# Second attention phase: the maxima's rows are transposed, copied and sent one position sooner in the pair ahead of theirs

## What is computed

```python
q = (x @ Wq.T + bq).reshape(b, l, h, hd).transpose(0, 2, 1, 3)      # k, v alike
scores = jnp.where(causal, jnp.einsum('bhqd,bhkd->bhqk', q, k) / math.sqrt(hd), -jnp.inf)
out = jnp.einsum('bhqk,bhkd->bhqd', jax.nn.softmax(scores, axis=-1), v)
return out.transpose(0, 2, 1, 3).reshape(b, l, d) @ Wo.T + bo
```

## Time and profile before

| | us |
|---|---|
| median of 3 runs | 1889.95 |
| lowest and highest run | 1889.94, 1899.09 |
| profiled execution, its own time | 1892.44 |
| span of the profiled execution | 1890.7 |
| PE busy in the span | 1665.3 (88%) |
| DVE, ACT, POOL busy | 1098.8, 861.6, 644.7 |
| mean granted TensorE clock | 0.947 of full |

### The profile page before, as it was taken

The page is one execution under the profiler, slowest core; times in us unless marked ns, Lnnn a source line. Parts: engine busy times, 40 slices in busy tenths (PEclk is TensorE's granted clock), DMA queues, the critical chain, the costliest instruction groups (busy, mean ns, idle before and its releaser), DMA issues. The chain is left out here.

```text
span 1890.7 us, 31907 instructions
## 1 busy us (share of the span) xinstructions
PE 1665.3 (88%) x10736; PEld 1162.3 (61%) x10736; DVE 1098.8 (58%) x2394; ACT 861.6 (46%) x1530; POOL 644.7 (34%) x1926
## 2 busy tenths in 40 slices
PE   4889988989986999999578899889889878999997
PEld 4555655655644777877455566566466446777785
DVE  5677677677763854545455655654654627554542
ACT  3456546555553544535234443443443426354441
POOL 4445545445440312213124433433433412131211
PEclk8899999999988999999789999899899898999998
DMA  2000110100105410110433533433443326211010
GB/s 102 2 13 14 41 30 13 35 24 13 35 24 168 128 67 12 55 67 1 150 48 49 78 57 68 75 51 68 74 63 63 52 86 193 70 37 67 0 45 23
DMA packets 78121, 106.97 MB, mean 57 GB/s; under 512 B 13195, under 2 KB 49675, under 8 KB 77973
## 3 DMA queue, kind: packets, MB, share of 16 engines
q1 hardware_dynamic: 77972, 105.10, 23.2%
HBM read 62.34 MB, written 16.78 MB: 42 GB/s over the span
## 5 line engine op out<-in xcount | busy, mean ns | idle before, releaser
L242 PE MATMUL f_ring<-xt,f_codes 128*128 128x512 f32 (+1 forms) x1408 | 362.6, 400 | 13.9 <-DVE f_codes L1519 7.9
L242 PEld LDWEIGHTS f_ring<-xt,f_codes 128*128 128x128 f32 (+1 forms) x1408 | 264.6, 189 | 84.0 <-issue 8.7
L1433 POOL TENSOR_TENSOR f_ht<-f_work,f_ht 128x512 fp32r<-128x512 f32 (+1 forms) x88 | 114.5, 1305 | 519.6 <-ACT f_ht L1491 519.6
L859 ACT ACTIVATE aa_region<-aa_scores 128x512 f32<-128x512 f32 x320 | 184.6, 599 | 83.5 <-PE aa_scores L1152 80.5
L859 ACT ACTIVATE ab_region<-ab_scores 128x512 f32<-128x512 f32 x320 | 181.4, 601 | 79.6 <-PE ab_scores L1152 79.1
L1576 DVE TENSOR_TENSOR f_work<-f_ring,f_work 128x512 f32<-128x512 f32 (+1 forms) x176 | 120.6, 690 | 139.8 <-ACT f_work L1480 117.2
L712 POOL TENSOR_SCALAR_AFFINE_SELECT ab_region<-ab_region 128x128 f32<-128x128 f32 x512 | 140.2, 297 | 176.7 <-ACT ab_region L859 176.2
L1480 ACT ACTIVATE f_work<-f_ring,f_scales 128x512 f32<-128x512 f32 (+1 forms) x176 | 120.6, 685 | 171.0 <-PE f_ring L242 170.5
L242 PE MATMUL f_ring<-f_dcodes,f_ht 128*128 128x512 f32 (+1 forms) x704 | 174.4, 402 | 9.7 <-DVE f_down_x L1546 9.2
L712 POOL TENSOR_SCALAR_AFFINE_SELECT aa_region<-aa_region 128x128 f32<-128x128 f32 x512 | 136.6, 295 | 91.8 <-ACT aa_region L859 91.4
L1112 PE MATMUL ab_maxima<-ab_stacks 96*128 96x128 bf16 (+3 forms) x512 | 144.9, 320 | 25.7 <-DMA ab_stacks<-ab_parted 13.4
(11 more groups left out here) (183 smaller groups left out, 2943.6 us busy)
## 6 DMA issues: line engine op xcount, KB each, us to landing
ab_stacks<-ab_parted SPq DMA_DIRECT2D x192, 128.0 KB, 4.2
f_raw<-mid SPq DMA_DIRECT2D x32, 256.0 KB, 4.4
f_x<-mid SPq DMA_DIRECT2D x28, 256.0 KB, 4.0
f_raw<-in_gate_q SPq DMA_DIRECT2D x10, 512.0 KB, 5.5
f_raw<-in_up_q SPq DMA_DIRECT2D x10, 512.0 KB, 4.6
f_raw<-in_down_q SPq DMA_DIRECT2D x10, 512.0 KB, 3.8
aa_x<-in_x SPq DMA_DIRECT2D x18, 256.0 KB, 2.8
ab_x<-mid SPq DMA_DIRECT2D x18, 256.0 KB, 3.0
```

Source lines behind the costliest of these rows:

```text
L242: mm = pe.matmul(out, w, x, start=start and i == 0, stop=stop and i == len(pairs) - 1)
L859: act.activation(probs[:, s // 2 % 2, SUB * (s % 2) + i, :], scores[:, sbk, :], ACT.Exp, scale=0.25).then_inc(scores_freed[sbk].sem, 1)
L1433: pool.tensor_tensor(ht[0:r, LO, n, :], hid[0:r, n % 2, :], ht[0:r, HI, n, :].bitcast(F32), ALU.subtract).then_inc(hid_lo.sem, 1)
```

## The change

In `ab` the positions at which the rows are transposed (PE), copied (DVE) and sent (SP) go from 2 to 1. In `aa` they stay at 2. No instruction is added or removed.

```diff
-        TRANSPOSE_AT, ROWS_AT, VALUES_AT = 2, 2, 4
+        TRANSPOSE_AT, ROWS_AT, VALUES_AT = (2, 2, 4) if rope else (1, 1, 4)
```

## The result

The changed kernel takes 1909.16 us in the median (1897.55 to 1914.72, 14 runs) against 1894.16 (1886.92 to 1899.76, 14 runs) before: ratio 1.0077, 95% interval [1.0062, 1.0092]. That is 0.8% slower, and outside the range of the prediction. The profiled execution took 1902.98 us, 10.5 more than that of before and the third quickest of the 14.

The account below looks back on a forecast made before the run. PE was taken to set the pace, with at most its 22.6 us wait for the maxima's rows removable. Step terms summed to +4.0 us, plus +2 for the clock: 1898.4 for the profiled execution, median 1896 us, range 1886 to 1906.

Parts of the forecast that it names:

- the low clock spreads: Rival: PE falls to the low clock in some eight steps with new or longer waits, 1907.6 us; chance 0.22.
- the term for the clock: Second attention phase: one or two more low-clock stretches at 1.7 us each, +2 us, bounds 0 to +14.
- the split's late steps: Steps such as 26: PE's earlier transposition waits for POOL's split of the maxima, +0.8 us each, +3.1 for four.
- the fourth-step term: Steps such as 31: the transposition falls into PE's waits for ACT's exponential or L925, -1.6 us.
- The second rival: Sends land with the rows, split never late: nearly all 22.6 us of rows' wait gained, 1868 to 1875; chance 0.07.
- The third rival: The sends land early and the split binds: +2.5 and -0.6 become +1.0 and -2.5, median 1892.5; chance 0.11.
- (1): Profile sign: PE's wait for the rows falls from 22.6 us to under 3.
- (2): Profile sign: L1112 waits for sends 1.5 to 2.5 us at steps 14, 18, 30, 34, 46, 50; sum some 15 to 20.
- (3): Profile sign: PE's wait at L1136 for POOL's split grows from 2 us to 10 or more, longest in step 10, 2.8.
- (4): Profile sign: SP issues the rows 1.0 to 2.1 us sooner in a unit's first step, 0.8 in its second.
- (5): Profile sign: PE's busy time is the same but for the clock.
- sign of being wrong: Either (2) stays small and batches get over 2 us shorter than 147, or the phase's granted clock falls below 0.93.

Follow-up runs that it names:

- e1: Changed kernel, but SP alone sends the rows at position 2 again, PE and DVE staying at 1: ratio 0.9948 to before, median 1883.3 us.
- e4: Changed kernel with the sends of position 1 moved to position 0 of the same step, ahead of the rows: ratio 0.9961 to before, median 1884.6 us.
- e6: Changed kernel with each unit's third steps left at position 2 on PE, DVE and SP: ratio 0.9996 to before, median 1889.9 us.
- e9: e1 with the third steps' transposition and copy also left at position 2: ratio 0.9893 to before, median 1870.3 us.
- e12: e9 with the early sends of e4: ratio 0.9865 to before, median 1867.7 us.
- e5: Kernel before with both the early first four sends of e13 and the moved first steps of e14: ratio 0.9871, median 1867.8 us.
- e15: Changed kernel with only the first four sends early, the last two still behind the second step's rows: ratio 1.0054 to before, median 1901.4 us.
- e7: Changed kernel, PE repeating position 0's scores matmul 8 times in each third step, where it waits for the sends: ratio 0.9961 to before, median 1884.3 us.
- e10: Control for e7: changed kernel with the same 8 repeats in each fourth step, where nothing waits: ratio 1.0205 to before, median 1929.1 us.
- e13: Kernel before with only the unit's first four sends early, rows left at position 2: ratio 0.9991, median 1889.7 us.
- e14: Kernel before with rows transposed, copied and sent at position 1 in each unit's first step alone, old sends: ratio 1.0010, median 1894.1 us.

## Why the prediction was wrong

The two waits that the prediction put in the place of the rows' wait, for the sends and for the split, both came, and the rival named "the low clock spreads", with a chance of 0.22, is what happened. The step that failed is the term for the clock, taken at +2 us for one or two more stretches: six more came, an estimated 8 to 10 us. The table sets the terms against the lengths of the steps in the two profiled executions (us, after less before).

| steps | predicted | measured | more at the low clock |
|---|---|---|---|
| 13+14, 29+30, 45+46 | +2.5 | +4.0, +1.1, +1.2 | 6.8, 0, 0 |
| 17+18, 33+34, 49+50 | -0.6 | -1.4, +0.2, -0.5 | -3.4, 0, 0 |
| 5+6, 21+22, 37+38, 53+54 | +1.3 | +1.6, +1.6, -0.1, -0.4 | 3.4, 3.4, 0, 0 |
| 9+10, 25+26, 41+42, 57+58 | +3.1 | +0.1, +0.6, +0.2, +1.4 | 0, 0, 0, 3.4 |
| 2, 60 to 62 | +2.6 | +2.4, +3.5 | 3.4, 3.4 |
| 0+1 | -1.0 | -1.5 | 0 |
| first steps such as 28 | -1.8 | -2.8 | 0 |
| steps 8 of a batch | -1.0 | +1.7, 0, 0, -1.6 | 3.4, 0, 0, -3.4 |
| fourth steps such as 31 | -1.6 + 0.5 | -1.8 | 0 |
| sum | +4.0 | +9.5 | 20.4 |

**The waits.** The entries of the table whose time at the low clock did not change sum to -3.6 us, where the prediction had some -0.3 for them; the nine others hold +13.1. So the sum of the waits was too high by about 3 us: the split's late steps cost 0.1 to 0.6 each where 0.8 stood, and the first steps gained 0.38 seven times. Terms were off the other way too: steps 30 and 46 cost 1.15 where 0.8 stood, and the fourth-step term missed that the transposition delays position 2 of steps 23, 39 and 55 (+0.5 each). That PE's idle time grew by 4.3 us beside a sum of +4.0 does not confirm the sum: idle time and step length are not the same, and of the -3.6 us only 1.4 are idle time. The time from position 1's scores in step 29 to k = 0 in step 30 was forecast at 6.1 us and is 6.15 (1235.19 to 1241.34).

**The clock.** Six more stretches of 3.4 us came, not one or two. Their price had been taken about right. Step 22 is 1.6 us longer than step 38, with the same waits and 3.4 us at the low level; step 14 is 2.7 longer than step 30 with 6.8. At these prices the 20.4 us more cost an estimated 8 to 10 us, nearly all of the phase's 9.5. I had argued from one step that a wait of 1.6 us leaves the clock alone, and the kernel before already had the counterexample: step 6 starts at 1017.26 after a wait of 1.66 us for the rows, and runs at 0.50 (PE alone, columns as in the earlier trace rows).

```profile
1017.50:1020.90 3.40, 3.40 (x19) 0.50 0.00 0
```

Step 26, which the prediction counted as agreeing with the Trainium skill on waits for DMA, has 0.6 us of such a wait and then 2.1 us of waits for DVE, so it speaks for waits of PE in general. After the change the wait for the sends is 2.4 to 2.7 us long in steps 14, 18, 30, 34, 46 and 50, and in nine of the other third steps (all but step 6) a wait for the split stands in the step, in seven of them behind one for the sends. Taking either away (e1 and e4, or e6) brings the low clock back to 52 to 53 us and with it 15 to 24 us of time. The Trainium skill says in "TensorE: Matmul & The Clock Gate", HAM oscillation, that a burst of matmuls between waits for DMA runs again at the low clock; step 14 after the change agrees, with 6.8 us at 0.50, and step 30, with the same wait, does not, so the rule gives no count.

**The median.** It lies 6 us above the profiled execution, where the prediction set it 2.5 below. Over the 14 runs the time goes roughly with the mean granted clock (1897.55 us at 0.940, 1914.72 at 0.934). A single profile can't tell this spread, and the range of 1886 to 1906 had room for the profiled execution but not for the median. Of the 13.2 us between 1896 and 1909.2, 4.2 are the start: the three runs of before had a median of 1889.95, the fourteen one of 1894.16. The other 9.0 are the change itself, forecast at 6 us and 15.0 in the medians (10.5 in the profiled pair).

**The second rival.** "The wait simply goes" was set at 1868 to 1875 and refused because the split would bind. That holds for the changed kernel with the sends in time (e1, 1883.3). That e9, e12 and e5 reach 1868 to 1870 does not speak for it: they leave the third steps' transposition at position 2, which it had not considered.

**The third rival** was priced at 1892.5, and e1 and e4, which are that case, came to ratios of 0.9948 and 0.9961, 1883 and 1885 us. In e1 steps 13+14, 29+30 and 45+46 cost the +1.0 us in sum that it had. The term that it missed is in steps 17+18, 33+34 and 49+50, set at -2.5 in sum: they fell by 2.6, 2.6 and 3.1 us, since with the waits of 2.2 to 2.9 us at the start of their second step went also the 3.4 us at the low clock that each of them had. The figure that the prediction took there from the Trainium skill, "DMA: Bandwidth & Descriptors", Anatomy of one DMA, is measured on that page on DMAs issued by GpSimd; these are SP's, and no run here shows a send from GpSimd.

**What the profile was to show.** (1) Rows' wait under 3: 0.9. (2) k = 0's wait 15 to 20 in six named steps: 15.2 there, and 13.3 more in the eight steps 6, 10, 22 and their like, 1.1 to 2.4 us each; I had this hidden under the split's wait, but it stands ahead of it. (3) Split's wait 10 or more: 12.9, the longest 2.0, in step 62, and not 2.8 in step 10. (4) Rows' issue 2.1 sooner in the first step: 4.3 us after the first send, where it was 6.5; right, but the two sends that it passed were left out. In the changed kernel they alone cost little (e15, 1901 us against 1909), because the last two bind. (5) PE's busy time the same but for the clock: 509.1 and 514.3. Neither sign of being wrong appeared: the granted clock of the phase is 0.933, just above the bound of 0.93 below which the forecast was to be given up, and the batches did not get shorter. That bound was too far off to warn.

**Open.** Which of two equal waits is followed by the low clock is not explained: nothing was found in the trace that tells step 14 from step 30 ahead of the fall, and in e6 it is the other of the two that falls. And e6's gain is put down to the clock by its numbers (idle -4.0, low clock -23.7, phase -13.3 us), but it was not run with fills.

## What to carry to other kernels

When an issuing queue works in order, a wait in it is a gate for everything behind: count, for every transfer that is moved, which others now stand behind its wait, in each step where it occurs, and not only in the one with the visible stall. Short waits of PE can cost more through the clock than through their length, and one step that got through such a wait at the high clock is no proof for the others: look at every step with a wait of that size. Where PE has to wait anyway, repeating a harmless matmul shows how much of a loss can hang on the clock, if the same repeats are also run where nothing waits and the part that lengthens the path is taken off.

## What the runs showed of the hardware

- Work of PE that has no use made the kernel faster: 28 us of repeated matmuls in 16 places took 20 us off the phase (e7), with the low clock down from 76.9 to 15.5 us. The same repeats where nothing waits cost 24 us (e10).
- Waits of the same length are followed by the low clock in one step and not in another: 1.66 us in step 6 and 1.57 in step 30 before, 2.43 in step 14 and 2.45 in step 30 after.
- Two changes to the order in SP's queue that each do nothing (e13, 0.9991, and e14, 1.0010) gave 0.9871 together (e5).
- Sends of 128 KB that follow each other land 0.8 to 1.2 us apart in a burst of eight, mostly 1.1, and the first 3.3 us after its issue; of the two that the changed kernel gives out 0.6 us apart into an empty queue the second lands 1.0 us behind the first (1240.29 and 1241.25). That spacing is what makes two more sends in the pile eat the 2.1 us that the first steps gain.
